# The first two groups of a down product in three rounded passes: one core, two transformer blocks

## The reference

```
def _L0_ffn_ref(x, w_gate, w_up, w_down):           # x: (4, 256, 256), hidden width 1024
    h = silu(x @ w_gate) * (x @ w_up)
    h_sparse = _sparsify_2to4(h)     # of every 4 neighbours, the 2 of greatest magnitude are kept
    return h_sparse @ w_down
x = x + attention0(layernorm(x))
x = x + _L0_ffn_ref(layernorm(x), ...)
x = x + attention1(layernorm(x))
x = x + ffn1(layernorm(x))           # the second block has a Hadamard transform in its feed-forward part
```

## Time and profile before

| | |
|---|---|
| time, median of 3 runs | 710.39 us (710.31 to 710.62) |
| profiled execution: time | 710.15 us |
| profiled execution: span of the trace | 708.4 us |
| instructions | 16161 |

### The profile page before, as it was taken

How to read it: one execution, slowest core, us unless ns; L and a number is a source line. 1 busy time by engine, 2 the same in 40 slices (tenths; PEclk the granted TensorE clock), 3 DMA queues, 4 the chain that set the end, 5 groups by cost and what they waited for, 6 DMA issues and landing times.

```text
span 708.4 us, 16161 instructions
## 1 busy us (share of the span) xinstructions
PE 691.2 (98%) x4468; PEld 624.6 (88%) x4468; DVE 526.0 (74%) x1662; ACT 451.4 (64%) x1738; POOL 347.9 (49%) x503
## 2 busy tenths in 40 slices
PE   5899999999999998999999999999999999999998
PEld 3789999999999997888878999999999999987887
DVE  6878888888898888969855776776676777796443
ACT  4788888788788885423257666666666666664221
POOL 4998888888788854002069841423232323016100
PEclk9999999999999999999999999999999999999999
DMA  6010210101021020100021010101010100000000
GB/s 237 2 46 20 87 47 1 46 0 45 1 104 59 1 75 1 46 0 1 16 89 61 1 61 2 61 3 58 20 40 37 67 0 0 0 2 1 1 31 30
DMA packets 9016, 24.76 MB, mean 35 GB/s; under 512 B 896, under 2 KB 3072, under 8 KB 8832
## 3 DMA queue, kind: packets, MB, share of 16 engines
q1 hardware_dynamic: 8240, 22.55, 9.2%
q10 hardware_dynamic: 720, 1.57, 0.6%
HBM read 23.07 MB, written 1.05 MB: 34 GB/s over the span
## 4 chain that ended last, share of the span: by engine, by line
PE 91%; DVE 4%; issue 2%; ACT 2%; POOL 1%; DMA 0%; ACTq 0%; POOLq 0%; DVEq 0%
PE bank L485 12%; PE bank L477 12%; PE bank L830 11%; PE bank L385 11%; PE bank L500 7%; PE bank L399 5%; PE bank L417 5%; PE bank L357 4%; PE bank L422 4%; PE bank L435 3%; PE bank L904 3%; PE bank L332 3%; PE bank L908 2%; PE bank L356 2%; PE bank L328 2%
## 5 line engine op out<-in xcount | busy, mean ns | idle before, releaser
L623 DVE SCALAR_TENSOR_TENSOR x<-bank,rinv,x 128x256 f32<-128x256 f32 x256 | 123.1, 481 | 25.9 <-PE bank L385 23.7
L601 ACT ACTIVATE probs<-scores,negmax 128x128 f32<-128x128 f32 (+1 forms) x256 | 116.6, 462 | 6.9 <-DVE negmax L661 4.1
L517 ACT CAST turned<-bank 128x256 fp32r<-128x256 f32 x104 | 38.8, 374 | 107.5 <-PE bank L399 103.2
L634 DVE TENSOR_TENSOR enc_lo<-bank,enc_hi 128x256 fp32r<-128x256 f32 x128 | 54.3, 424 | 47.9 <-PE bank L357 29.4
L725 POOL TENSOR_TENSOR a_hi<-raw_a,zero 128x384 fp32r<-128x384 f32 (+1 forms) x60 | 43.6, 727 | 84.5 <-PE bank L500 84.5
L385 PE MATMUL bank<-b_hi,enc_hi 128*128 128x256 f32 x256 | 73.5, 287 | 0.0
L642 DVE TENSOR_TENSOR turned<-bank,turned 128x256 fp32r<-128x256 f32 x104 | 43.7, 420 | 40.1 <-ACT probs_t L518 40.1
L286 POOL TENSOR_TENSOR ln_r<-ln_ve,neg_half 128x1 f32<-128x1 f32 x24 | 15.8, 658 | 115.0 <-DVE ln_ve L264 115.0
L385 PE MATMUL bank<-b_hi,enc_lo 128*128 128x256 f32 x256 | 72.1, 282 | 0.0
L385 PE MATMUL bank<-b_lo,enc_hi 128*128 128x256 f32 x256 | 72.0, 281 | 0.0
L738 POOL TENSOR_TENSOR rms_r<-meansq,neg_half 128x3 f32<-128x3 f32 x64 | 55.1, 860 | 29.8 <-DVE meansq L712 27.4
(11 more groups left out here) (171 smaller groups left out, 2337.0 us busy)
## 6 DMA issues: line engine op xcount, KB each, us to landing
raw_a<-in_wa SPq DMA_DIRECT2D x10, 768.0 KB, 4.5
raw_a<-in_wa SPq DMA_DIRECT2D x9, 512.0 KB, 4.5
raw_b<-in_wb SPq DMA_DIRECT2D x16, 256.0 KB, 2.6
x<-in_x SPq DMA_DIRECT2D x4, 256.0 KB, 5.5
hid_last<-in_wax SPq DMA_DIRECT2D x2, 512.0 KB, 5.1
w_a<-in_w2t SPq DMA_DIRECT2D x1, 1024.0 KB, 4.8
raw_b<-in_wdown SPq DMA_DIRECT2D x2, 512.0 KB, 3.8
raw_a<-in_wa ACTq DMA_DIRECT2D x1, 512.0 KB, 4.9
```

What stands on the lines that cost most here:

```text
L601: nc.scalar.activation(probs[:, c % 4, c0:c1], scores[:, c % 2, c0:c1], ACT.Exp, bias=negmax[:, c % 2, r:r + 1], scale=-1.0, accum_out=row ...
L623: nc.vector.scalar_tensor_tensor(out=x[:, m % 8, :], in0=output_bank(m)[:, hh * D:(hh + 1) * D], scalar=rinv[:, u, r:r + 1], in1=x[:, m % ...
L634: nc.vector.tensor_tensor(enc[1][:, w % 2, dst], bank[O_BANK][:, 0:D], enc[0][:, w % 2, dst].bitcast(F32), ALU.subtract).then_inc(s["elo"], 1)
```

## The change

For groups 0 and 1 the down product is done in three rounded passes; group 2 and the last group stay as they are. ScalarE copies the raw down weights into the main parts `b_w[t][0]` (`act_down_hi`, 128x1024 each) and the kept hidden values into `encf[0]`, two tiles `j` at a time (`act_kept_hi`, 128x1024). GpSimd subtracts for the remainders `b_w[t][1]` and `encf[1]`, six subtractions of 128x1024 (`pool_ffn0`, `pool_kept_lo`), ahead of its four powers. TensorE runs 12 products of 128x256 for each tile, all four `j` of one pass before the next pass, and in the first tile waits for the remainders only ahead of the third pass. It no longer waits for the keeps but for the main parts and the weights. Group 1's main parts wait until down product 0 is done, since there is one `encf`. On VectorE the two keeps of group 1 move ahead of the adds of group 0's tiles 0 and 1.

```
         pe_down:
-                    if f == 0:
+                    if f == 0 and k == 2:
                         pe.wait_ge(s["hs"], 4 * k + 4)
-                        if k < 2:
-                            pe.wait_ge(raw_bs[0][t], 16 * 5)
+                    elif f == 0:
+                        pe.wait_ge(s["hi"], 4 * k + 4)
+                        pe.wait_ge(s_down_hi, t + 1)
+                        pe.wait_ge(s_down_lo, t + 1)
...
-                if f == 0:
+                if f == 0 and k == 2:
                     for j in range(4):
                         mm = pe.matmul(...)   # unchanged: fp32, 4 products
+                elif f == 0:
+                    for q, ((l, r), j) in enumerate([(p, j) for p in PASSES for j in range(4)]):
+                        if tt == 0 and l == 1:
+                            pe.wait_ge(s["lo"], 4 * k + j + 1)
+                        mm = pe.matmul(bank[6 + d % 2][:, 0:D], encf[l][:, j, tt * P:(tt + 1) * P],
+                                       b_w[t][r][:, j * D:(j + 1) * D], start=q == 0, stop=q == 11)
...
+        def act_down_hi(act, t):
+            act.wait_ge(raw_bs[0][t], 16 * 5)
+            act.wait_ge(at[0]["op"], UNITS)
+            nc.scalar.copy(b_w[t][0][:, :], raw_b[:, t, :]).then_inc(s_down_hi, 1)
+
+        def act_kept_hi(act, k, half):
+            act.wait_ge(ff[0]["hs"], 4 * k + 2 * half + 2)
+            if half == 0 and k:
+                act.wait_ge(ff[0]["down"], 4 * k)
+            js = slice(2 * half, 2 * half + 2)
+            nc.scalar.copy(encf[0][:, js, :], hidden(0, k, js)).then_inc(ff[0]["hi"], 2)
+
+        def pool_kept_lo(pool, k):
+            for half in range(2):
+                pool.wait_ge(ff[0]["hi"], 4 * k + 2 * half + 2)
+                js = slice(2 * half, 2 * half + 2)
+                nc.gpsimd.tensor_tensor(encf[1][:, js, :], hidden(0, k, js), encf[0][:, js, :].bitcast(F32),
+                                        ALU.subtract).then_inc(ff[0]["lo"], 2)
+
+        def pool_ffn0(pool):
+            for t in range(2):
+                pool.wait_ge(s_down_hi, t + 1)
+                nc.gpsimd.tensor_tensor(b_w[t][1][:, :], raw_b[:, t, :], b_w[t][0][:, :].bitcast(F32),
+                                        ALU.subtract).then_inc(s_down_lo, 1)
+            pool_kept_lo(pool, 0)
+            pool_kept_lo(pool, 1)
+            for t in range(4):
+                ln_pool(pool, 2, t)
...
         act_ffn0:
             for i in range(4):
                 act_abs(act, i)
+            act_down_hi(act, 0)
             for k in range(3):
                 i = 4 * (k + 1)
                 act_silu(act, 0, i)
                 if k == 0:
                     ln_act(act, 1, 7, 7)
+                elif k == 1:
+                    act_kept_hi(act, 0, 1)
                 act_silu(act, 0, i + 1)
+                if k == 0:
+                    act_down_hi(act, 1)
                 act_silu(act, 0, i + 2)
                 act_abs(act, i)
                 act_abs(act, i + 1)
-                if k == 2:
+                if k == 1:
+                    act_kept_hi(act, 1, 0)
+                elif k == 2:
                     act_next_a(act)
                 act_silu(act, 0, i + 3)
                 act_abs(act, i + 2)
+                if k < 2:
+                    act_kept_hi(act, k, k)
                 act_abs(act, i + 3)
...
         dve_ffn0:
-                if k == 1:
-                    for tt in range(4):
-                        dve_xadd(dve, 0, 0, tt)
-                if k < 2:
+                if k == 0:
                     dve_keep(dve, k, 0)
                     dve_keep(dve, k, 1)
+                elif k == 1:
+                    for tt in range(4):
+                        if tt < 2:
+                            dve_keep(dve, k, tt)
+                        dve_xadd(dve, 0, 0, tt)
```

More of the change, by code:

```diff
@@ L222, in build @@
         s_late, s_late_hi, s_late_lo = (sem("late_columns_" + n) for n in ("loaded", "high", "low"))
+        s_down_hi, s_down_lo = sem("down0_high"), sem("down0_low")
         s_bf, s_hadmm, s_hadev = (sem(n) for n in ("butterfly", "had_product", "w2_made"))
@@ L1491, in _ @@
             pool_drain0(pool)
-            for t in range(4):
-                ln_pool(pool, 2, t)
+            pool_ffn0(pool)
             slots(pool, 1, pool_slot, pool_head, pool_tail(pool, 1))
```

## The result

The changed kernel took 717.98 us (median of 4 runs, 717.39 to 718.84), the kernel before 710.38 us on the same chip (4 runs, 710.31 to 710.62). The ratio is 1.0107, with a 95% interval of 1.0095 to 1.0119: 7.6 us slower. The forecast was 715.2 us with a range up to 717.4. The sign and every wait of TensorE that the walk named are there, with nearly the sizes that it gave them; the time is 2.8 us above the forecast and 0.6 above the range.

A forecast was written before the change was run, and what follows sets the result against it. TensorE, busy 98% of the span, was taken to bound the kernel. New waits of 7.05 us less 2.28 saved gave +4.8 on 710.39, so 715.2 us; likeliest case 713.3 to 717.0, wider range 710.9 to 717.4.

The forecast's parts named there:

- the walk: Step through VectorE and GpSimd turns from the weights to group 1, at 2.40 us a remainder: TensorE waits 7.05 us.
- What TensorE saves: Down products of groups 0 and 1: each takes 5.99 us in place of 7.13, 2.28 us saved in all.
- What ScalarE gets: Six copies of 128x1024 at 1.05 us, 6.3 us together, in ScalarE's idle time at no cost.
- What they do to VectorE: The deciding term: VectorE's instructions with two SBUF inputs and GpSimd's subtractions wait for each other, whole instructions long.
- The question without a row: Whether a two-input VectorE instruction waits for GpSimd; no trace row showed it, and the prediction took it that it does.
- rival "hidden": Two-input VectorE instructions don't wait for GpSimd, compares stay at 1.22 us, TensorE never waits: 708.1 us, chance 0.15.
- Gate product 8: TensorE's gate product that needs hidden(5), held up behind the weights' subtractions: begins at 300.6, 0.35 us late.
- tile 2 of group 0: Third tile of down product 0, waiting for VectorE's add of the first tile: starts at 316.9, TensorE waits 5.3 us.
- tile 2 of group 1: Third tile of down product 1, waiting for the first tile's add: starts at 332.3 for 330.9, TensorE waits 1.4 us.
- The order of turns: VectorE and GpSimd alternate when both want SBUF; if VectorE kept its turn, the walk would give +3.7 us.
- the counts don't need the same path: Bound: if uint16 counts needn't share the compares' path, the 2.1 us behind weights 1 go, giving +2.9 us.
- The sum: 0.35 + 5.3 + 1.4 = 7.05 us of new waits, less 2.28 saved: +4.8 us, a time of 715.2 us.

The follow-up runs named there:

- the kernel with small subtractions: The changed kernel with its six GpSimd subtractions cut to 128x2 each, nearly all remainders left out: 708.03 us, ratio 0.9969.
- The run with fills: The changed kernel with each GpSimd subtraction replaced by two GpSimd zero fills of the same 128x1024, remainders left out: 707.99 us, ratio 0.9967.
- the pieces: The changed kernel with each GpSimd subtraction of 128x1024 cut into four of 128x256: 713.96 us, ratio 1.0054.
- the run with TensorE kept busy: The changed kernel with 20 unused products of 128x512 on TensorE ahead of tile 2 of group 0: 715.61 us, ratio 1.0077.
- The run with the adds first: The changed kernel with each residual add before the keep in group 1's phase, not behind it: 716.9 us, ratio 1.0095.

## Why the prediction was right in its waits and wrong in its time

**What TensorE saves: right.** 2.28 us was taken; the kernel with small subtractions is 2.28 us faster than before.

**What ScalarE gets: right.** The same kernel has all six copies and shows no cost.

**What they do to VectorE: right, and shown by experiments.** The question without a row was whether an instruction with two SBUF inputs waits for GpSimd. It does: 2.50 us where 1.22 was the rule, and 1.22 again with the subtractions made small. The rival "hidden" (708.1) is out: it needed compares of 1.22 us beside GpSimd's work, and that is seen only with fills in place of the subtractions. The Trainium skill, "SBUF — State Buffer", section "SBUF: two separate sides", restricts the lock for two-input instructions to a GpSimd instruction that reads SBUF. The run with fills agrees, with compares of 1.21 us beside fills of 0.96.

**The walk: right in its places, a little short in its sizes.** Gate product 8 was 0.35 us late by the walk and 0.51 in the trace, tile 2 of group 0 waited 5.3 and 5.33, tile 2 of group 1 1.4 and 1.61. The order of turns was as taken: GpSimd, compare, GpSimd, compare. The bound "the counts don't need the same path" falls with the 2.38 us of the count at 297.43, and for the counts with two inputs with the 0.95 us beside the pieces. These errors and the small lags come to 0.6 us in the profiled execution, and the median of the run with TensorE kept busy is 0.4 us above the forecast.

**The sum: this is the step that failed.** It was written as "0.35 + 5.3 + 1.4 = 7.05 us of new waits, less 2.28 us", after "TensorE sets the time to the end as before". A wait was priced at its length. The prediction read the clock row, 9 tenths or more throughout, and gave the clock no term and no bound. In that trace TensorE never waits for longer than 0.93 us once it has its first operands, so the row says nothing of a long wait. The one long wait of that trace, the 6.9 us at its start, did show the price, not in the clock row but in the pace of the products behind it, 0.43 us each in place of 0.23. The missing term is 1.42 us in the profiled execution (1.3 without the restart), and 2.4 us in the median by the difference to the run with TensorE kept busy. The profiled execution is the cheapest of the four in this: its mean granted clock is 0.998, that of the other three, 717.87 to 718.84 us, is 0.995. Those three have no timeline. The run with the adds first has one at a mean clock of 0.994, and there tiles 2 and 3 lost 2.2 us.

A range with a bound for the clock, even only "the tiles behind the wait at half speed", 2.88 us, would have reached to 717.0 + 2.9 = 719.9 and held the time. The other error, 0.6 us in the sizes of the walk, lies within the stated bounds.

**What stays open.** How much of the 2.4 us is the start-up isn't known exactly. The profiled execution of the changed kernel is a late one: its first compare starts at 291.69, where the kernel before and the six variants that leave the work ahead of it unchanged have it between 290.92 and 291.59, and the run with TensorE kept busy has it at 291.04. Of the 1.88 us between these two executions (717.39 and 715.51), 0.65 are the start-up and 1.3 are tiles 2 and 3. So the price of the clock behind the wait is 1.3 us where the mean clock is 0.998 and about 2.2 us where it is 0.994; that the three others with 0.995 paid the latter is an inference from the mean clock. Why the clock comes back sooner in one execution than in another, and why it falls behind 2.0 us in two of ten, no run here shows.

## What to carry to other kernels

Before work is given to an idle engine, look at what it shares with the engine that is nearly full: here six instructions of GpSimd that looked hidden took 17.7 us of its own free time and stopped the busiest helper of TensorE for whole instructions. The busier engine, at half the duration and with nobody to wait for, was the better place. And where a change makes TensorE wait for microseconds, price the wait at its length plus the work behind it at the lower clock; a clock row at full speed throughout doesn't show that price. Look for the longest wait in the trace, the one at the start too, and at how far apart the products behind it are.

## What the runs showed of the hardware that wasn't expected

- The granted clock fell behind waits of 5.2 and 4.1 us in all eight executions of these two kernels (mean clock 0.994 to 0.998). Behind the wait of 2.8 us of the run with pieces the mean clock was 0.998 in two executions of four and 1.000 in the profiled one; where it fell in the two isn't shown. Behind a wait of 2.0 us it fell in two of ten. Around the wait of 1.46 us in group 1 of the changed kernel it stayed at 1.00 (330 to 350 us).
- Tiles 2 and 3 behind the wait lost 1.3 us in one execution (mean clock 0.998) and 2.2 us in another, of the kernel with the adds first (0.994).
- At the start of an execution the first products of 128x512 are 0.43 us apart in place of 0.23, until 12.5 us in one and 13.5 us in another, with a clock row that reads 1.00.
- TensorE doing useless products through a wait made the kernel 2.4 us faster than leaving it idle.
- A GpSimd fill held a count with one uint16 input on VectorE (0.63 us for 0.29, seen once) and does not hold a compare with two f32 inputs (1.21 us).
- When both engines want the path, turns alternate by instruction, also with pieces of 128x256: nine compares then take 1.44 us in the mean.
